# A wider share for GpSimd in the experts, and an earlier second band in attention

## The reference

```
u  = layernorm over channels of x
y  = x + proj( window attention( instance norm(u) * norm_w + norm_b ) )   # 4 heads of 8, windows of 8x8
t  = y as tokens (8 x 4096 tokens of 32 channels)
z  = layernorm over channels of t
p  = softmax(z @ router_w + router_b); the two best of 8 experts, weights divided by their sum
out = t + sum over the two of p_e * (z @ expert_w[e] + expert_b[e])
```

## Time and profile before

| | |
|---|---|
| median of 3 runs | 382.94 us (381.27 to 383.5) |
| the profiled execution | 381.23 us |
| its span, first to last instruction | 379.3 us |
| mean granted TensorE clock | 0.976 |
| PE busy | 333.4 us (88%) |
| DVE busy | 327.5 us (86%) |
| ACT busy | 274.8 us (72%) |
| POOL busy | 163.6 us (43%) |

### The profile page before, as it was taken

The page is one execution under the profiler, slowest core; times in us unless marked ns, Lnnn a source line. Parts: engine busy times, 40 slices in busy tenths (PEclk is TensorE's granted clock), DMA queues, the critical chain, the costliest instruction groups (busy, mean ns, idle before and its releaser), DMA issues.

```text
span 379.3 us, 12902 instructions
## 1 busy us (share of the span) xinstructions
PE 333.4 (88%) x5494; PEld 176.7 (47%) x5494; DVE 327.5 (86%) x422; ACT 274.8 (72%) x477; POOL 163.6 (43%) x191
## 2 busy tenths in 40 slices
PE   7999889999999868989989998989988878858895
PEld 2556556666656534655655654546542212111221
DVE  2599988998998975999998896899898999999884
ACT  3668768779878865787877987876765785566763
POOL 8610000221222120378545212068759448957653
PEclk9999999999999996999999999999999998898999
DMA  7700011011010000101101101075222653773482
GB/s 297 334 3 3 3 31 29 3 31 29 3 32 29 4 14 17 29 2 31 29 3 30 32 2 29 21 174 118 49 65 62 162 129 78 166 182 83 118 210 94
DMA packets 13385, 26.19 MB, mean 69 GB/s; under 512 B 1680, under 2 KB 3856, under 8 KB 12944
## 3 DMA queue, kind: packets, MB, share of 16 engines
q1 hardware_dynamic: 12752, 23.60, 23.7%
q10 hardware_dynamic: 576, 1.77, 1.2%
HBM read 5.96 MB, written 4.19 MB: 27 GB/s over the span
## 4 chain that ended last, share of the span: by engine, by line
PE 50%; DVE 22%; ACT 8%; issue 7%; POOL 6%; DMA 5%; SPq 0%; POOLq 0%; DVEq 0%; ACTq 0%
PE psum L689 13%; PE psum L708 7%; PE psum L674 6%; DVE neg_max L1309 4%; PE psum L716 4%; PE psum L658 3%; PE psum L592 3%; PE psum L869 3%; DVE window_work L1312 3%; PE psum L487 2%; DMA stage<-in_x 2%; PE psum L640 2%; DVE window_work L1466 2%; DVE o_tok L1320 2%; PE psum L859 1%
## 5 line engine op out<-in xcount | busy, mean ns | idle before, releaser
L369 POOL TENSOR_TENSOR o_norm<-o_tok,o_rden 128x128 f32<-128x128 f32 x64 | 25.4, 419 | 169.2 <-DVE o_rden L1322 169.2
L1013 ACT ACTIVATE probs<-psum 128x512 f32<-128x512 f32 x128 | 74.7, 596 | 23.8 <-PE psum L689 23.1
L689 PE MATMUL psum<-weights_sb,window_work 128*128 128x128 f32 x512 | 81.2, 286 | 9.4 <-ACT k_sb L989 5.5
L1309 DVE TENSOR_REDUCE neg_max<-psum 128x16 f32<-128x1024 f32 x64 | 76.8, 1199 | 9.1 <-PE psum L674 9.1
L1312 DVE TENSOR_TENSOR window_work<-psum,neg_max 128x1024 f32<-128x1024 f32 x64 | 78.4, 1225 | 2.2
L689 PEld LDWEIGHTS psum<-weights_sb,window_work 128*128 128x128 f32 x512 | 55.4, 142 | 40.1 <-issue 16.0
L708 PE MATMUL psum<-probs,v_cols 128*32 128x64 f32 x2048 | 52.4, 226 | 0.4 <-DVE o_tok L1320 0.2
L708 PEld LDWEIGHTS psum<-probs,v_cols 128*32 128x32 f32 x2048 | 34.1, 110 | 30.2 <-issue 15.6
L996 ACT ACTIVATE stage<-k_sb,weights_sb 128x512 f32<-128x512 f32 x64 | 44.2, 723 | 0.0
L674 PE MATMUL psum<-stage 32*64 32x256 f32 x1024 | 35.9, 386 | 7.0 <-DVE window_work L1312 4.3
L1320 DVE STREAM_TRANSPOSE o_tok<-psum 128x512 f32<-128x512 f32 x32 | 22.8, 712 | 14.5 <-PE psum L708 14.5
(11 more groups left out here) (143 smaller groups left out, 618.4 us busy)
## 6 DMA issues: line engine op xcount, KB each, us to landing
stage<-act_all SPq DMA_DIRECT2D x36, 256.0 KB, 4.4
out<-v_cols SPq DMA_DIRECT2D x16, 256.0 KB, 2.1
stage<-in_x SPq DMA_DIRECT2D x3, 1024.0 KB, 13.3
x_moved<-x_cur SPq DMA_DIRECT2D x14, 192.0 KB, 2.4
gate_rows<-gate_parts SPq DMA_DIRECT2D x16, 128.0 KB, 2.9
x_moved<-x_cur SPq DMA_DIRECT2D x14, 64.0 KB, 2.2
weights_sb<-weights ACTq DMA_DIRECT2D x1, 811.5 KB, 13.9
stage<-in_x SPq DMA_DIRECT2D x1, 768.0 KB, 6.0
```

Of the source, the lines that this page charges most:

```text
L369: last = pool.tensor_tensor(o_norm[:, hf, :, p * 16:p * 16 + 16].rearrange("p g (b d) -> p g b d", b=2), t[:, p * 8:p * 8 + 8, :].rearrang ...
L689: last = nc.tensor.transpose(bank[TURN_BANKS[v % 2]][:, b * P:b * P + P], heads.rearrange("p h k -> p (h k)"), const["c_ident"][:, :])
L1013: nc.scalar.activation(probs[:, w % 4, :], bank[TURN_BANKS[w % 2]][:, :], ACT.Exp).then_inc(exp_done, 1)
L1309: nc.vector.tensor_reduce(m_t, t, AX.X, ALU.max, negate=True).then_inc(max_done, 1)
```

## The change

In the experts, for chunks 1 to 10, GpSimd's share of a half goes from 512 to 640 columns (`WIDE`), ScalarE copies 640 columns for it from banks 2 and 3, and VectorE multiplies banks 4 and 5 (1024 columns) first and then the other 384 columns of bank 3, after waiting for ScalarE's copy. TensorE computes pair 1 first and pair 0 second there. The SBUF copies of the gates are the two halves of one new tensor; k_sb shares it. The other chunks keep their form.

In attention, `queries_keys(m + 1)` comes one weighing sooner in chunks 1 to 14. `instance_affine(1)` moves from the end of VectorE's chunk 6 to between its two shifts of the second half of that chunk, and `current(8)` from the head of ScalarE's chunk 7 to the end of chunk 6.

```diff
+WIDE = 5 * CHUNK // 4
...
-        q_sb = sb("q_sb", [P, CHUNK])
-        k_sb = sb("k_sb", [P, CHUNK])
+        gate_flat = sb("gate_flat", [P, 2 * WIDE])
+        k_sb = gate_flat[:, 0:CHUNK]
...
-        gate_copy = [q_sb, k_sb]
+        gate_copy = [gate_flat[:, 0:WIDE], gate_flat[:, WIDE:2 * WIDE]]
...
+        def pool_cols(c):
+
+            return WIDE if 1 <= c <= 10 else CHUNK
...
             def scale(c, eh):
 
                 if eh == 0:
-                    wait_tokens(pool, c, 1)
+                    wait_tokens(pool, c, 1 if pool_cols(c) == CHUNK else 2)
                 pool.wait_ge(gate_copied, c * 2 + (eh + 1))
                 wait_past(pool, y_step, c * 2 + eh - 1)
-                pool.tensor_tensor(scaled[eh][:, 0, :], x_rep[:, slot(c), 0, :], gate_copy[eh][:, :],
+                n = pool_cols(c)
+                pool.tensor_tensor(scaled[eh].rearrange("p b n -> p (b n)")[:, 0:n],
+                                   x_rep[:, slot(c), :, :].rearrange("p b n -> p (b n)")[:, 0:n], gate_copy[eh][:, 0:n],
                                    ALU.mult).then_inc(pool_scaled, 1)
...
                         turn(m - 1, NW - 1)
+                        queries_keys(m + 1)
                         weigh(*before, NW - 3)
-                        queries_keys(m + 1)
                         weigh(*before, NW - 2)
...
             def gate_pair(c, eh, pair):
 
+                first_pair = 0 if pool_cols(c if eh == 1 else c - 1) == CHUNK else 1
                 if pair == 0:
                     wait_past(pe, gate_copied, c * 2 + eh)
-                    wait_past(pe, scaled_done, c * 4 + (2 * eh - 1))
-                else:
-                    wait_past(pe, scaled_done, c * 4 + 2 * eh)
+                wait_past(pe, scaled_done, c * 4 + (2 * eh - 1 if pair == first_pair else 2 * eh))
...
-                    gate_pair(c, eh, 0)
+                    first_pair = 0 if pool_cols(c) == CHUNK else 1
+                    gate_pair(c, eh, first_pair)
                     if eh == 0 and c + REP_FIRST >= CHUNKS:
                         bias(c)
-                    gate_pair(c, eh, 1)
+                    gate_pair(c, eh, 1 - first_pair)
...
                 for hf in range(2):
                     n, back = (m, 4) if hf == 1 else (m - 1, NW)
                     behind = not (first and hf == 0)
-                    if hf == 0 and m + 1 == BANDS:
-                        current(m + 1)
...
                     if hf == 1 and not first:
                         keep_projection(m - 1)
+                    if hf == 1 and m + 2 == BANDS:
+                        current(m + 2)
...
             def copy_gates(c, eh):
 
-                act.wait_ge(gate_ps, c * 4 + (2 * eh + 1))
+                act.wait_ge(gate_ps, c * 4 + (2 * eh + (1 if pool_cols(c) == CHUNK else 2)))
                 wait_past(act, pool_scaled, c * 2 + eh - 1)
-                nc.scalar.activation(gate_copy[eh][:, :], bank[2][:, :], ACT.Copy).then_inc(gate_copied, 1)
+                n = pool_cols(c)
+                nc.scalar.activation(gate_copy[eh][:, 0:n], psum[:, 2:4, :].rearrange("p b n -> p (b n)")[:, 0:n], ACT.Copy
+                                     ).then_inc(gate_copied, 1)
...
                 for hf in range(2):
                     shift(m, hf, 0)
+                    if hf == 1 and m == BANDS - 2:
+                        instance_affine(1)
                     if not first:
                         turn_back(m - 1, hf)
...
-                        elif m == BANDS - 2:
-                            instance_affine(1)
...
+                    else:
+                        dve.wait_ge(gate_ps, c * 4 + (2 * eh + 1))
+                        nc.vector.tensor_tensor(scaled[eh][:, 2:4, :], x_rep[:, slot(c), 2:4, :], psum[:, 4:6, :],
+                                                ALU.mult).then_inc(scaled_done, 1)
+                        dve.wait_ge(gate_copied, c * 2 + (eh + 1))
+                        nc.vector.tensor_tensor(scaled[eh][:, 1, WIDE - CHUNK:CHUNK], x_rep[:, slot(c), 1, WIDE - CHUNK:CHUNK],
+                                                bank[3][:, WIDE - CHUNK:CHUNK], ALU.mult).then_inc(scaled_done, 1)
```

More of the change, by code:

```diff
@@ L1461, in _ @@
                     wait_past(dve, y_step, c * 2 + eh - 1)
-                    dve.wait_ge(gate_ps, c * 4 + (2 * eh + 1))
-                    nc.vector.tensor_tensor(scaled[eh][:, 1, :], x_rep[:, slot(c), 1, :], bank[3][:, :],
-                                            ALU.mult).then_inc(scaled_done, 1)
-                    dve.wait_ge(gate_ps, c * 4 + (2 * eh + 2))
-                    nc.vector.tensor_tensor(scaled[eh][:, 2:4, :], x_rep[:, slot(c), 2:4, :], psum[:, 4:6, :],
-                                            ALU.mult).then_inc(scaled_done, 1)
+                    if pool_cols(c) == CHUNK:
+                        dve.wait_ge(gate_ps, c * 4 + (2 * eh + 1))
+                        nc.vector.tensor_tensor(scaled[eh][:, 1, :], x_rep[:, slot(c), 1, :], bank[3][:, :],
+                                                ALU.mult).then_inc(scaled_done, 1)
+                        dve.wait_ge(gate_ps, c * 4 + (2 * eh + 2))
+                        nc.vector.tensor_tensor(scaled[eh][:, 2:4, :], x_rep[:, slot(c), 2:4, :], psum[:, 4:6, :],
+                                                ALU.mult).then_inc(scaled_done, 1)
+                    else:
+                        dve.wait_ge(gate_ps, c * 4 + (2 * eh + 1))
+                        nc.vector.tensor_tensor(scaled[eh][:, 2:4, :], x_rep[:, slot(c), 2:4, :], psum[:, 4:6, :],
+                                                ALU.mult).then_inc(scaled_done, 1)
+                        dve.wait_ge(gate_copied, c * 2 + (eh + 1))
+                        nc.vector.tensor_tensor(scaled[eh][:, 1, WIDE - CHUNK:CHUNK], x_rep[:, slot(c), 1, WIDE - CHUNK:CHUNK],
+                                                bank[3][:, WIDE - CHUNK:CHUNK], ALU.mult).then_inc(scaled_done, 1)
                     if (c, eh) == (0, 0):
```

## The result

The median went from 381.97 us (11 runs, 380.33 to 383.50) to 379.40 us (11 runs, 377.44 to 381.04): ratio 0.9931, 95% interval 0.9902 to 0.9959, so faster by 0.7%. The forecast was 377.8 from 382.94, a ratio of 0.987. The direction and the range held; the gain, 2.6 us, is about half of the 5.1 that was forecast.

What follows compares the result with a forecast made beforehand. TensorE and VectorE were taken as nearly full in attention and the experts, with one large TensorE hole in attention. Terms -4.5, -0.4 and -0.2 (experts) sum to -5.1 us, 376.1 profiled, forecast 377.8; range 374.6 to 380.8.

Steps and rivals of the forecast that it cites:

- Term 1: Attention, chunks 6 and 7: affine and x_cur of the second image group sooner, so the reduction at 151.01 comes 4.5 us sooner.
- the earlier trace's two cases: TensorE after idling: 1.20 us left four transposes at full clock, 2.80 us slowed eight products; 1.9 us taken nearer the first.
- Term 2: Attention, chunks 1 to 14: queries and keys one weighing sooner shorten TensorE's 0.25 us waits; at most 2.5 us, taken -0.4.
- Terms 3 and 4: Experts, chunks 1 to 10: VectorE's shorter multiplications win 2.7 us; longer GpSimd operations and ScalarE copies cost 1.3.
- term 4: Experts: GpSimd's longer multiplications keep the third quad's gates about when they came, losing part of VectorE's gain; +1.3 us.
- the 0.4 us between -0.6 and -0.2: Experts: terms 3 to 6 summed to -0.6; -0.2 was taken, for chance meetings of the two engines.
- Term 5: Order inside an expert half: chunk 9's first copy about 0.9 us later, delaying an exponential; 0.66 comes back; +0.3 us.
- Term 6: End of experts: GpSimd's longer part delays the fourth quad's last gate operation, which frees SP's copies for chunk 13; +0.5 us.
- Blocking decides: Rival: VectorE's gate operations on SBUF wait for longer GpSimd multiplications; experts +5.4 instead of -0.2, 383.4 us; chance 0.05.
- The clock stays low: Rival: the shorter stop in attention still drops TensorE to 1.2 GHz; attention gives 2.46, 379.9 us; chance 0.17.
- VectorE keeps all: Rival: in the experts terms 4 to 6 are hidden, so -2.7 us there; 375.3 us; chance 0.15.
- x_cur isn't sooner: Rival: the moved affine or a late transfer keeps chunk 8's x_cur late; attention gives at most 1, 381.7 us; chance 0.08.

Runs made afterwards that it cites:

- order_only: The whole change with its new order in chunks 1 to 10, but GpSimd keeps 512 columns as before; ratio to before 0.9917.
- after_exp_first: The changed kernel with ScalarE's exponential of quad 3's gates moved ahead of the copy of half 18; ratio to before 0.9910.
- narrow_vector: As order_only, but VectorE multiplies only 384 columns, leaving 128 columns of one image out in chunks 1 to 10; ratio to before 0.9870.
- experts_only: The change's expert part alone, attention as in before; ratio to before 1.0084.
- swap_only: Before with only queries_keys one weighing sooner; ratio to before 0.9997.
- attn_only: Before with both attention edits, experts unchanged; ratio to before 0.9880, timed a second time at 0.9854.

## Why the prediction was right and where it was wrong

**Term 1, -4.5.** Right in its chain of causes; its size depends on the clock. The reduction came at 145.12, 5.89 sooner; 0.86 of that was there already in chunk 6 (0.64 by the swap, 0.2 from the first stage of the kernel), so the move gave 5.0. The wait was forecast at 1.9 and was 1.82, the affine's cost of at most 1.4 was about 0.9, x_cur was forecast at 137.27, which less the 0.86 is 136.4, and started at 136.30. What I took as settled between the earlier trace rows's two cases, the clock behind the wait, is not: it differs between executions of kernels with the same wait. With the low stretch the move gives 3.6 (the reduction at 146.69, less 0.74 that was there before) and the whole of attention 5.0; without it they give 5.0 and 6.65. The forecast of 4.9 for the whole fits the more frequent case, but by luck: term 1 was 0.9 too large there and term 2 1.0 too small. I had given the low clock a chance of 0.17, and it came in seven of ten traces.

**Term 2, -0.4.** Undersized in the trace: 1.4. I had counted waits of the ten chunks with such a row and taken nearly nothing of 2.5. The gain isn't spread over them: it comes in chunks 5, 6, 11 and 12, at 0.3 to 0.4 us each, and the earlier trace rows's 0.25 was worth nothing in the others. Alone it can't be shown by the times.

**Terms 3 and 4, sizes of the operations.** Right: 546 ns against 0.544 us, 704 against at most 743 ns for the copy, and GpSimd's operation of 640 columns 1.54 to 1.56 us where it runs free, 1.64 on average. As a price they aren't confirmed. Together they said -1.4 us; from order_only to after the ratio goes up by 0.0014, some 0.5 us, which the intervals can't tell from nothing. What term 4 rested on didn't come: in after no wait of TensorE for gate rows is left where before has 0.32, and the lead at the second half of chunk 8 is 6.66, as it was at the start of the experts (6.65), where terms 3 and 4 had 0.6 more. Its real cost was the holds, some 2 us, for which the sum had only the 0.4 us between -0.6 and -0.2.

**Term 5, +0.3, is the step that failed.** It said: "Between halves with gate work that is covered", and looked for the one place where it isn't. order_only puts the price of the order at 0.6% (0.9917 against 0.9854), 2.4 us. At the named place the mechanism was right: the gate copy of chunk 9's first half starts 2.47 us after VectorE's first multiplication (332.04) instead of 1.25, so 1.22 later where 0.9 was forecast, and the wait for the exponential grew by 1.07. The 0.66 that I took back came at that operation (0.20 us, 0.79 before) and was lost at others. What the term missed is that the loss goes on through chunks 8 to 10. By the code, the first pair of a half may be written once VectorE's first operation of the half before is done; before, that left the 1.21 us of the 1024 columns as cover for those two products, in the new order only the last operation's 0.68 or 0.54. That this lack of cover is the cause isn't shown: at order_only's wait of 1.60 us the banks were free long before, and TensorE was late by its own work at the low clock. How the 2.4 us divide between the exponential, the products and the clock stays open.

**Term 6, +0.5.** Undersized. The wait for chunk 13's copy grew by 0.71, and the operation that sets it free, at 348.24, came 4.47 sooner than before's while the lead at the third quad's gates had been over 6. Two of that chain's operations, L1407 and L1412, were held: 1.38 and 1.26 us, against 0.68 and 1.08.

**The rivals.** *Blocking decides* named the right sign for the expert part and a part of its cause: holds exist (L1373, L1407, L1412, together some 1.9 us of VectorE's time), and by the sums above they take back most of what the width saves, but the order costs without any longer GpSimd operation. The Trainium skill, "SBUF — State Buffer", section "Who interferes with whom", has GpSimd exclude VectorE operations with two SBUF inputs, or in a two-port mode. The traces agree: L1407, with two SBUF inputs, took 1.38 us beside a GpSimd multiplication instead of 0.68, the 128x64 operation of after_exp_first, with one input, 1.57 us beside GpSimd's 1.54 (whether it ran in a two-port mode no run shows), while the multiplications that read PSUM kept 1210 ns. *The clock stays low* was half true: the low stretch came in most executions, but the move still gave 3.6, not 2.46. *VectorE keeps all* was wrong: by narrow_vector, even free of cost only some 1.8 of 2.7 arrive. *x_cur isn't sooner* was wrong: 136.30.

**The sum.** Attention -1.2 to -1.5% (4.6 to 5.6 us; forecast 4.9), experts +0.8% (3.2 us by experts_only; forecast -0.2). The forecast missed by the expert part; that it stayed in the range is owed to the range's width of 6 us. The forecast's base of 382.94, the median of three runs, was also 1.0 above the later median of before.

**Open.** How the price of the width divides into ScalarE's and GpSimd's longer operations wasn't tried apart, nor was the new order in some of the chunks alone, so which part of chunks 8 to 10 makes it costly isn't known.

## What to carry to other kernels

When an engine's work is split in pieces that other engines feed, the order of the pieces is what hides the feeding; changing it so that another engine can take a larger share may cost more than the share is worth (here 2.4 us for about nothing), and one kernel with the new order and the old shares shows it. Work on a transfer's input is best moved into idle time just before it is needed, and the gain is read at the next stage boundary, not at the wait. Before a wait is blamed for a loss, take it away alone: here it turned into a hold of about the same length.

## What the runs showed of the hardware

The granted clock after a wait of 1.4 to 1.9 us of TensorE was 1.00 throughout in three traced executions and at the 1.2 GHz level for 3.4 us in seven, with the same work before and behind it; after waits of 4.0 us (before, experts_only) and 4.4 us (swap_only) it was at that level for about 6.8 and 3.4 us. And executions of one program differ by such stretches: attn_only ran 375.12 us at a mean granted clock of 0.984 and 378.65 at 0.964. At 2 x (1 - clock) x span that is 11.9 and 27.1 us at the low level, so 15.2 us more of it cost 3.5 us, 0.23 us for each. A comparison of two traced executions can be off by that much, which is why the verdicts above are from the timed runs and the traces serve for mechanisms.

A VectorE operation on 128x8 took 0.23 us at 131.15 of after with GpSimd idle, and 1.31 in before beside a GpSimd addition of 1.27 us: where small operations stand can matter more than how many there are.
